# Attention stage: softmax row sums taken from the exponentials' accumulator output, repeated on GpSimd and transposed on TensorE

## What is computed

```python
q = split_heads(q_x @ Wq) / math.sqrt(C_HID)      # q_x is the group-normalised x
k = split_heads(kv_x @ Wk)
v = split_heads(kv_x @ Wv)
a = jnp.einsum('bnhqc,bnhkc->bnhqk', q, k)
a = a + mask_bias + tri_bias
a = jax.nn.softmax(a, axis=-1)
o = jnp.einsum('bnhqk,bnhkc->bnhqc', a, v)
g = jax.nn.sigmoid(q_x @ Wg).reshape(lead + (H, C_HID))
o = o * g
return o @ Wo                                      # heads put side by side first
```

## Time and profile before

| | |
|---|---|
| median of three runs | 4865.68 us |
| the profiled execution's own time | 4870.61 us |
| its span in the trace | 4868.7 us |
| attention stage in the span | about 99 to 1970 us, 256 rows |
| busy over the span: PE, DVE, ACT, POOL | 4478.4, 3429.5, 2818.1, 2617.0 us |
| mean granted TensorE clock | 0.957 of full speed |

### The profile page before, as it was taken

The page is one execution under the profiler, slowest core; times in us unless marked ns, Lnnn a source line. Parts: engine busy times, 40 slices in busy tenths (PEclk is TensorE's granted clock), DMA queues, the critical chain, the costliest instruction groups (busy, mean ns, idle before and its releaser), DMA issues. The chain is left out here.

```text
span 4868.7 us, 107582 instructions
## 1 busy us (share of the span) xinstructions
PE 4478.4 (92%) x35750; PEld 3338.1 (69%) x35750; DVE 3429.5 (70%) x10053; ACT 2818.1 (58%) x6302; POOL 2617.0 (54%) x2043
## 2 busy tenths in 40 slices
PE   6999999999999999766999989999749996999995
PEld 5777777777777777525677757777423445999995
DVE  6888888888888888532566656666428995567665
ACT  0888888888888888202333333333324663666665
POOL 0999999999999999102232322333105551122222
PEclk8999999999999999878999999999869998999997
DMA  7222222222222222795222221222556887999994
GB/s 307 67 75 75 73 74 75 75 75 74 73 74 75 75 75 72 268 390 183 68 68 67 69 85 64 69 68 67 207 214 205 279 276 242 265 290 293 292 291 130
DMA packets 803938, 713.79 MB, mean 147 GB/s; under 512 B 60693, under 2 KB 700692, under 8 KB 794839
## 3 DMA queue, kind: packets, MB, share of 16 engines
q1 hardware_dynamic: 784875, 673.53, 45.3%
q10 hardware_dynamic: 14717, 20.01, 1.2%
q0 software_dynamic: 3808, 13.47, 0.7%
HBM read 507.48 MB, written 199.29 MB: 145 GB/s over the span
## 5 line engine op out<-in xcount | busy, mean ns | idle before, releaser
L309 POOL TENSOR_TENSOR at_bias<-at_tri,at_mask 128x1024 f32<-128x1024 f32 x512 | 1215.1, 2374 | 28.3 <-DMA at_mask<-in_L_conv_mask_bias_dram 11.7
L427 ACT ACTIVATE at_probs<-at_neg_s,at_neg_max 128x256 f32<-128x256 f32 x2048 | 871.2, 505 | 0.7 <-DVE at_neg_max L478 0.7
L478 DVE CUSTOM_DVE_ANT_0 at_neg_s<-at_p_s,at_bias 128x256 f32<-128x256 f32 x2048 | 759.9, 418 | 7.6 <-PE at_p_s L350 2.9
L301 POOL TENSOR_TENSOR at_paired_t<-at_probs_t 128x512 f32<-128x512 f32 x512 | 655.9, 1281 | 9.2 <-ACT at_probs_t L419 5.0
L361 PE MATMUL at_p_t<-all_ident,at_probs 128*128 128x128 f32 x4096 | 628.2, 276 | 0.6 <-DVE at_probs_t L486 0.4
L946 ACT ACTIVATE ml_h<-ml_p,l_b 128x512 f32<-128x512 f32 x384 | 263.9, 687 | 555.6 <-PE ml_p L905 555.6
L361 PEld LDWEIGHTS at_p_t<-all_ident,at_probs 128*128 128x128 f32 x4096 | 476.0, 141 | 131.7 <-issue 104.2
L1047 POOL TENSOR_TENSOR ml_x2t<-ml_z,ml_xb 128x512 f32<-128x512 f32 x128 | 163.8, 1280 | 735.2 <-DVE ml_z L1013 735.2
L1967 POOL TENSOR_TENSOR dw_room<-dw_room,all_b_plain 128x512 f32<-128x512 f32 x128 | 179.4, 1402 | 592.1 <-DMA dw_room<-x3t 592.1
L914 PE MATMUL ml_p<-l_w1s,ml_h 128*128 128x128 f32 x4096 | 478.4, 275 | 0.8 <-issue 0.8
L914 PEld LDWEIGHTS ml_p<-l_w1s,ml_h 128*128 128x128 f32 x4096 | 467.8, 192 | 3.1 <-issue 3.1
(11 more groups left out here) (230 smaller groups left out, 9252.1 us busy)
## 6 DMA issues: line engine op xcount, KB each, us to landing
dw_xw<-planes SPq DMA_DIRECT2D x128, 528.0 KB, 4.7
sp_xs<-x SPq DMA_DIRECT2D x128, 512.0 KB, 8.9
dw_wts<-patch_w SPq DMA_DIRECT2D x128, 512.0 KB, 6.2
planes<-pw_plane SPq DMA_DIRECT2D x128, 264.0 KB, 3.2
in_xs<-in_x_dram SPq DMA_DIRECT2D x32, 1024.0 KB, 7.7
at_xs<-in_x_dram SPq DMA_DIRECT2D x256, 128.0 KB, 2.4
at_kvs<-in_L_conv_kv_x_dram SPq DMA_DIRECT2D x256, 128.0 KB, 2.7
at_mask<-in_L_conv_mask_bias_dram SPq DMA_DIRECT2D x256, 128.0 KB, 3.2
```

Source lines behind the costliest of these rows:

```text
L301: pool.tensor_tensor(paired_t[:, n % 2, part], probs_t[:, n % 3, part, 0], probs_t[:, n % 3, part, 1], ALU.add).then_inc(paired, 1)
L309: pool.tensor_tensor(bias[:, n % 2, part], tri[:, part], mask[:, n % 4].unsqueeze(1).broadcast_to((128, 4, COLS)), ALU.add).then_inc(maske ...
L427: e = act.activation(probs[:, h, qh, :], neg_s[:, n % 2, h, qh, :], ACT.Exp, bias=neg_max[:, n % 2, i:i + 1], scale=-1.0)
L478: t = dve.tensor_tensor_reduce(neg_s[:, n % 2, h, qh, :], p_s[h][:, qh, :], bias[:, n % 2, i, :], -1.0, 3.0e38, ALU.add, ALU.min, neg_max[ ...
```

## The change

The exponentials' instruction is given an accumulator output, `accum_out`, into a new tile `sums` (one column for each half of the queries and head), so that the row sums come with queries on the partitions. `pair` goes away. In its place POOL copies `sums` into a new tile `spread` in which each sum stands 32 times (`spread_sums`, one instruction a row, 128x256), between the two `add_mask` of the iteration. In `weigh`, the four matmuls by ones are replaced by two transposes of 128x128 of `spread` into the same place in PSUM. `weigh` now begins on `even_read` and `odd_read`, and waits for `sums_spread` between the values' matmuls and the transposes. The exponentials get one more wait, for `sums_spread` of two rows before, since `sums` is a ring of 2. The tile of ones, its memset and the semaphore `cleared` go.

```diff
         @block.gpsimd
         def _(pool):
-            pool.memset(ones[:, :], 1.0).then_inc(cleared, 1)
             pool.wait_ge(const_loaded, 16 * 6)
 
-            def pair(n, half):
-                pool.wait_ge(even_read, 2 * n + half + 1)
-                pool.wait_ge(odd_read, 2 * n + half + 1)
+            def spread_sums(n):
+                pool.wait_ge(exped, (n + 1) * HEADS)
                 if n >= 2:
                     pool.wait_ge(weighed, n - 1)
-                part = slice(2 * half, 2 * half + 2)
-                pool.tensor_tensor(paired_t[:, n % 2, part], probs_t[:, n % 3, part, 0], probs_t[:, n % 3, part, 1],
-                                   ALU.add).then_inc(paired, 1)
+                pool.tensor_copy(spread[:, n % 2], sums[:, n % 2].unsqueeze(3).broadcast_to((128, HALVES, HEADS, HEAD_DIM))
+                                 ).then_inc(sums_spread, 1)
...
             for n in range(-2, rows + 2):
-                for half in range(2):
-                    if exists(n - 1):
-                        pair(n - 1, half)
-                    if exists(n + 2):
-                        add_mask(n + 2, half)
+                if exists(n + 2):
+                    add_mask(n + 2, 0)
+                if exists(n - 1):
+                    spread_sums(n - 1)
+                if exists(n + 2):
+                    add_mask(n + 2, 1)
...
             def weigh(n):
-                pe.wait_ge(paired, 2 * n + 2)
+                pe.wait_ge(even_read, 2 * n + 2)
+                pe.wait_ge(odd_read, 2 * n + 2)
...
-                for h in range(HEADS):
-                    mm = pe.matmul(p_out[HEAD_DIM * h:HEAD_DIM * (h + 1), 1, :], ones[:, :], paired_t[:, n % 2, h, :],
-                                   start=True, stop=True)
+                pe.wait_ge(sums_spread, n + 1)
+                for half in range(HALVES):
+                    mm = pe.transpose(p_out[:, 1, half * 128:(half + 1) * 128],
+                                      spread[:, n % 2, half].rearrange("p h d -> p (h d)"), ident[:, :])
                 mm.then_inc(weighed, 1)
...
                 act.wait_ge(biased, n * HEADS + h + 1)
                 if n >= 1:
                     act.wait_ge(p_turned, (n - 1) * HEADS + h + 1)
+                if n >= 2:
+                    act.wait_ge(sums_spread, n - 1)
                 for qh in range(HALVES):
                     i = h * HALVES + qh
                     e = act.activation(probs[:, h, qh, :], neg_s[:, n % 2, h, qh, :], ACT.Exp,
-                                       bias=neg_max[:, n % 2, i:i + 1], scale=-1.0)
+                                       bias=neg_max[:, n % 2, i:i + 1], scale=-1.0,
+                                       accum_out=sums[:, n % 2, qh, h:h + 1])
                 e.then_inc(exped, 1)
```

More of the change, by code:

```diff
@@ L215, in attention @@
         wq_s, wk_s, wv_s, wg_s, wo_s = (weights[:, i, :] for i in range(5))
-        ones = m.sb("ones", [128, HEAD_DIM])
         tri = m.sb("tri", [128, HEADS * HALVES, COLS])
@@ L232, in attention @@
         probs_t = m.sb("probs_t", [128, 3, HEADS, HALVES, COLS])
-        paired_t = m.sb("paired_t", [128, 2, HEADS, COLS])
+        sums = m.sb("sums", [128, 2, HALVES, HEADS])
+        spread = m.sb("spread", [128, 2, HALVES, HEADS, HEAD_DIM])
         og = m.sb("og", [128, 2, COLS])
@@ L240, in attention @@
         p_out = m.ps("p_out", [128, 2, COLS])
-        const_loaded, cleared = m.sem("const_loaded"), m.sem("cleared")
+        const_loaded = m.sem("const_loaded")
         x_loaded = [m.sem(f"x_loaded{i}") for i in range(8)]
@@ L249, in attention @@
         masked, scored, biased, exped = (m.sem(n) for n in ("masked", "scored", "biased", "exped"))
-        p_turned, even_read, odd_read, paired = (m.sem(n) for n in ("p_turned", "even_read", "odd_read", "paired"))
+        p_turned, even_read, odd_read, sums_spread = (m.sem(n) for n in ("p_turned", "even_read", "odd_read", "sums_spread"))
         weighed, den_made, den_step, gated = (m.sem(n) for n in ("weighed", "den_made", "den_step", "gated"))
@@ L387, in _ @@
             pe.wait_ge(const_loaded, 16 * 6)
-            pe.wait_ge(cleared, 1)
             for n in range(-2, rows + 2):
```

## The result

Over 22 runs of each, the kernel before has a median of 4864.3 us and the changed kernel one of 4818.82 us. The ratio is 0.9898, with a 95% interval of 0.989 to 0.9906. It leaves out six executions of either kernel that took some 70 to 80 us more, in a later stage as far as a trace shows, and two of the changed kernel that took 6657.19 and 17722.89 us; the medians of the rest are 4863.4 and 4814.4 us. On the 4865.68 us that the prediction started from, that is 4816 us, with 4815 predicted.

A forecast was written before the change was run, and what follows sets the result against it. PE was taken as the attention stage's bound: 0.22 us saved a row, less 0.02 for ties, gives 0.20 over 253 rows, 51 us. From the 4865.68 us median that makes 4815 us, range 4785 to 4950 us.

The forecast's parts named there:

- PE is the bound, POOL just under it, ACT third: Attention stage: PE's work sets the 7.23 us row period; POOL has 0.06 us idle a row, ACT 1.04 us.
- PE saves 0.22 us a row: In `weigh` on PE, 0.55 us of matmuls by ones becomes 0.11 form change plus 0.22 for two transposes.
- rival 2: ACT's read is hidden and L333's small wait falls too: PE saves up to 0.31 us a row, 4788 us; chance 0.10.
- POOL's copy costs 764 ns, covered: On POOL, the 128x256 copy takes 764 ns; work falls from 7.17 to 5.4 us, covering up to 1.6 us more.
- A read of the accumulator costs x = 0.09 us: On ACT, each of eight exponentials a row takes 0.09 us more, bounds 0 to 0.20 us.
- ACT's work is 6.19 us, it has 1.04 us to pass, so x decides at 0.13: ACT, per row: above 0.13 us added per exponential ACT becomes the bound; chance 0.30, 5008 us at 0.20.
- 0.15 us of room: Gate on DVE to PE's L383: the 0.91 us gap shrinks by 0.54 and 0.22 us but stays positive.
- a loop of handovers through ACT: Stated failure condition: PE's period set by handovers through ACT, which eight longer exponentials would stretch; no size given.
- late copy: PE's new wait for `sums_spread` comes late; POOL's copy would have to be some 7 us late; chance 0.01.
- rival 4: Attention stage's clock falls to 1.2 GHz, adding some 7 us a row, about 6640 us in all; chance 0.01.
- Rival 3: With ACT's added cost between 0.12 and 0.13 us per exponential, the time stays within 10 us of 4866; chance 0.08.
- allowance of 0.02 us for many ties: Added to the row period for many ties at once, taking it from 7.01 to 7.03 us.

The follow-up runs named there:

- the halved pairs: Kernel before, with POOL's pair additions cut to half their columns: ratio 1.0003.
- the accumulator alone: Kernel before, with its exponentials also giving out their accumulator into a tile nobody reads: ratio 1.0002.
- the transposes with and without POOL's relief: Kernel before with two transposes replacing the four matmuls by ones: ratio 0.9941; with POOL's pair additions also cut to half their columns: 0.9889.
- the kernel with the new order on PE: Changed kernel with values' copy on DVE, PE's scores directly behind the weighing, DVE's denominator after the kv copy and first bias before the gate: ratio 1.0692.
- the kernel with more work: Changed kernel with one small 128x1 ACT copy behind each head's exponentials, four a row: ratio 1.0067.

## Why the prediction was right

The forecast's mechanism held: PE set the period before and after, and saved what its sum said. One step beside it, the room on ACT, was wrong, and that the time came out right there was luck.

- *PE is the bound, POOL just under it, ACT third.* Shown, by the halved pairs (no change), the accumulator alone (no change) and the transposes with and without POOL's relief (7.12 and 7.02 us).
- *PE saves 0.22 us a row.* Measured 0.21. The four matmuls' 0.55 us became 0.12 of form change (the weighing now takes 1.00 us to its successor rather than 0.88) and 0.27 us for two transposes, not 0.22. The transposes of the probabilities behind them take 0.44 us rather than 0.49. The sum of my step came out; its split did not quite, since the surcharge of the first transposes after a change of form moved with the change. The 1.08 us from the scores to L331, of which I took up to 0.09 us for a true wait, are unchanged, and they are no wait: in the kernel with the new order on PE the scores are followed by the transposes of the sums, which need nothing of DVE's copy of kv, and the distance is again 1004.78 - 1003.70 = 1.08 us. So the 0.31 us of rival 2 were not there to be had.
- *POOL's copy costs 764 ns, covered.* It costs 399 ns, half of it, and was covered. Twice too dear a price changed nothing.

```profile
L298 POOL COPY at_spread<-at_sums x229: 388/399/420, 299.9 to 1899.6; 128x256 f32<-128x256 f32 x115
```

- *A read of the accumulator costs x = 0.09 us.* Measured 0.09, in every row. The term that I could only bound, 0 to 0.20, was right because the read behaves as the smallest ACT instruction does: 0.195 us long against 0.203, with about 0.1 us of it hidden by the overlap. The small copies of the kernel with more work, 0.20 us long, add 0.09 us to the chain too. DVE's free read the earlier trace rows was the wrong model for ACT.
- *ACT's work is 6.19 us, it has 1.04 us to pass, so x decides at 0.13.* This step was off, in two ways. The first is the reading of idle time. The profile counts it from the end of the record before, but without a wait the next instruction starts 0.11 us before that end. Rows of ACT in the kernel before:

```profile
1004.37 0.59 ACT L419 ACTIVATE at_probs_t<-at_p_t 128x512 f32<-128x512 f32 x1
...
1008.93 0.58 ACT L419 ACTIVATE at_probs_t<-at_p_t 128x512 f32<-128x512 f32 x1
1010.25 0.39 ACT L441 ACTIVATE at_queries<-at_p_in 128x256 f32<-128x256 f32 x1 [0.74 <-PE at_p_in L334]
```

  The values start at 1005.22. The distances from copy to successor are 0.85 and 1.32 us, where 0.48 is enough, so the room was 0.37 + 0.84 = 1.21 us, ACT's own work was 6.0 us before the change and 6.73 after it, and by that alone x could have been (7.23 - 6.0) / 8 = 0.15. The second way is the loop through the gate and the first bias. It holds all eight exponentials and is 6.99 us long at x = 0.09, so it reaches 7.23 at x = 0.09 + 0.24 / 8 = 0.12. I had followed ACT's delay to the gate and from there to L383 on PE, and found 0.15 us of room up to its weight load. That was about right: the gate ends at 1004.70 and the weight load starts at 1004.83.

```profile
1004.83 0.53 PEld L383 LDWEIGHTS at_p_out<-at_weights,at_og 128*128 128x128 f32 x4
```

  I had not followed it to what stands behind the gate on DVE. That loop and PE's bound come out nearly equal, 6.99 and 7.02 us, and nothing in the prediction foresaw it. That the time was right in spite of this was luck. The prediction did name a loop of handovers through ACT as what would make it wrong, but did not look for one.
- *The clock and the late copy.* In the traces of the changed kernel the granted clock of the attention stage stayed at 1.00 with 22 transposes a row and four matmuls fewer. The rule in the Trainium skill, "TensorE: Matmul & The Clock Gate", Part 4, that transposes do not count as busy time in the way that matmuls do, changed nothing in them. But one of the 22 executions of the changed kernel took 6657.19 us, with a mean granted clock of 0.638 where the others have 0.94 to 0.96. That is near the 6640 us of rival 4. No trace of it was kept, so neither the stage in which the clock fell is known nor whether the change has a part in it; none of the 81 executions of the kernel before on record took more than 4947.3 us. The execution of 17722.89 us had a mean granted clock of 1.00, so the clock does not explain that one, and its cause is open too.
- *Rival 3, the gain lost in the ties.* It needed x between 0.12 and 0.13, and x is 0.09. The allowance of 0.02 us for many ties was hardly spent: 7.02 against 7.01.

## What to carry to other kernels

When two engines are both nearly full, relieving either alone tells little: here one relief gave nothing, the other half, and both together all. A change that moves work to a third engine should be followed not only to the first consumer that becomes late, but to whatever stands behind that consumer in its engine's order. The sum around the loop must stay under the period, as well as each engine's own sum. And the room of an engine is more than its idle time in the profile, by the overlap of neighbouring records at each wait, here 0.11 us.

## What the runs showed of the hardware

- Giving out the accumulator on ACT adds an instruction ACTIVATION_READ_ACCUMULATOR of 195 ns for each exponential, which adds 0.09 us to the chain behind a 128x256 exponential; the exponential itself lasts the same 505 ns. On DVE the counterpart of 0.08 us adds nothing measurable.
- A POOL copy that reads each of 8 columns 32 times and writes 128x256 takes 399 ns, less than the 412 ns of the copy of 128x128 in the earlier trace rows. Columns alone don't give the price of a POOL copy.
- In the kernel with the transposes alone, the only one in which POOL shows no idle time, the record of the same mask addition is 3108 ns long and not 2374 as in the changed kernel. The starts are as far apart as before: the pair additions follow the mask additions by 2.33 us in both timelines. So the duration of a POOL record is not its cost. Why it grows was not tested.
- The 16 records of the scores (32-row form) take 1.08 us to the next matmul, the 16 of the weighing (32-column form) 1.00 us when a full-array one follows. In the single records of the changed kernel's trace, four start together, and the step from one four to the next is 0.22 us in both. The step out of the form is 0.32 us from the scores and 0.33 from the weighing, so leaving costs 0.11 us in either. The difference lies at the start: the first step inside the form is 0.32 us in the scores and 0.24 in the weighing.
